# Steps of a fused long-convolution block: order of four engines where the pipeline has no FFN, on one core

## The reference

```python
def _L0_attn_ref(u, ...):                    # u: 2 x 4096 x 256, already layer-normed
    z = rmsnorm(u, pre_norm_w) @ in_proj_w.T     # then a causal depthwise conv of 3 taps
    x2, x1, v = jnp.split(z_pre, 3, axis=1)
    xv = x1 * v                                  # a long convolution along the 4096 rows
    y = (yconv + xv * D_skip[None, :, None]) * x2
    y = y @ out_proj_w.T + u
    zm = rmsnorm(y, post_norm_w)
    mlp = jax.nn.gelu(zm @ l1_w.T) * (zm @ l2_w.T) @ l3_w.T     # 672 hidden
    return y + mlp
def _L0_ffn_ref(x, W1, b1, W2, b2, scale):
    # m1, m2: outer products of rows 1 to 16 of each batch, added to W1 and W2
    h = einsum(x, W1) + scale * einsum(x, m1) + b1              # 1024 hidden
    h = jax.nn.gelu(h, approximate=False)
    return einsum(h, W2) + scale * einsum(h, m2) + b2
x = x + _layernorm(_L0_attn_ref(_layernorm(x)))
x = x + _layernorm(_L0_ffn_ref(_layernorm(x)))
```

## Time and profile before

| | |
|---|---|
| median of 3 runs | 1122.17 us (1121.68 to 1126.74) |
| profiled execution | 1130.82 us, span 1129.1 us |
| mean granted TensorE clock in it | 0.974 |
| ACT table loads | 64 |

### The profile page before, as it was taken

The page is one execution under the profiler, slowest core; times in us unless marked ns, Lnnn a source line. Parts: engine busy times, 40 slices in busy tenths (PEclk is TensorE's granted clock), DMA queues, the critical chain, the costliest instruction groups (busy, mean ns, idle before and its releaser), DMA issues.

```text
span 1129.1 us, 25540 instructions
## 1 busy us (share of the span) xinstructions
PE 1058.1 (94%) x9280; PEld 1026.8 (91%) x9280; DVE 880.7 (78%) x2313; ACT 724.5 (64%) x1607; POOL 295.2 (26%) x560
## 2 busy tenths in 40 slices
PE   4999999798678999999999999988999999999996
PEld 4899998576568999999999999988999999999996
DVE  7998998654368788888778888788778888877774
ACT  6888887555455666666666666565666566666553
POOL 6677674630010112111112111111111211111121
PEclk9999999889688999999999999998999999999999
DMA  3333321997743233443333344452333333333000
GB/s 123 114 122 118 108 75 39 273 252 196 136 78 66 38 57 48 51 56 66 57 57 48 49 53 65 90 123 38 59 55 57 49 49 52 56 62 57 26 14 29
DMA packets 108926, 89.23 MB, mean 79 GB/s; under 512 B 7121, under 2 KB 103537, under 8 KB 108545
## 3 DMA queue, kind: packets, MB, share of 16 engines
q1 hardware_dynamic: 107632, 85.16, 36.8%
q0 software_dynamic: 672, 2.39, 0.6%
q10 hardware_dynamic: 496, 0.05, 0.0%
HBM read 62.12 MB, written 17.07 MB: 70 GB/s over the span
## 4 chain that ended last, share of the span: by engine, by line
PE 66%; DVE 6%; DMA 4%; issue 3%; ACT 1%; POOL 1%; ACTq 0%; SPq 0%; DVEq 0%; POOLq 0%
PE ps_ring L1393 35%; PE ps_w L1393 14%; PE ps_m L1393 9%; PE ps_o L1393 3%; DMA toep<-taps_scratch 3%; PE ps_rt L1403 2%; PE ps_y L823 2%; PE ps_y L832 1%; DVE base L1249 1%; POOL sc L1017 1%; PE ps_m L1439 1%; DVE bn L1155 1%; PE ps_s L801 0%; DVE prod L1197 0%; DVE pt_l L1167 0%
## 5 line engine op out<-in xcount | busy, mean ns | idle before, releaser
L1017 POOL TENSOR_TENSOR sc<-sc,neg_half 128x2 f32<-128x2 f32 x128 | 95.5, 746 | 738.4 <-DVE sc L1348 449.7
L1077 ACT ACTIVATE gate<-ps_ring 128x256 f32<-128x256 f32 x192 | 73.2, 382 | 137.3 <-PE ps_ring L1393 136.2
L1393 PE MATMUL ps_ring<-mt_h,wl_h 128*128 128x256 f32 x640 | 130.6, 287 | 6.4 <-ACT mt_h L1144 6.4
L1393 PE MATMUL ps_ring<-mt_l,wl_h 128*128 128x256 f32 x640 | 130.3, 286 | 6.4 <-DVE mt_l L1167 6.4
L1098 ACT ACTIVATE hid<-ps_ring,b1s 128x256 f32<-128x256 f32 x256 | 114.0, 491 | 31.7 <-PE ps_w L1393 13.9
L1393 PE MATMUL ps_ring<-mt_h,wl_l 128*128 128x256 f32 x640 | 130.1, 286 | 0.0
L1167 DVE TENSOR_TENSOR ht_l<-hid,ht_h 128x256 fp32r<-128x256 f32 x256 | 103.2, 423 | 15.4 <-ACT ht_h L1102 9.5
L1393 PEld LDWEIGHTS ps_ring<-mt_h,wl_h 128*128 128x128 f32 x640 | 101.5, 196 | 7.7 <-ACT mt_h L1144 4.4
L1393 PEld LDWEIGHTS ps_ring<-mt_l,wl_h 128*128 128x128 f32 x640 | 101.3, 196 | 7.6 <-DVE mt_l L1167 7.6
L1393 PE MATMUL ps_ring<-xt_h,we_h 128*128 128x256 f32 x512 | 102.6, 282 | 2.3 <-DVE prod L1197 1.5
L1197 DVE TENSOR_TENSOR prod<-ps_ring,gate 128x256 f32<-128x256 f32 x192 | 80.9, 421 | 29.6 <-ACT gate L1077 25.7
(11 more groups left out here) (179 smaller groups left out, 2772.2 us busy)
## 6 DMA issues: line engine op xcount, KB each, us to landing
toep<-taps_scratch SPq DMA_DIRECT2D x30, 512.0 KB, 4.9
xa<-in_x SPq DMA_DIRECT2D x16, 512.0 KB, 4.5
x_scratch<-x2c SPq DMA_DIRECT2D x16, 512.0 KB, 3.5
x2s<-x_scratch SPq DMA_DIRECT2D x32, 256.0 KB, 6.9
xa_c<-in_x SPq DMA_DIRECT2D x32, 256.0 KB, 2.7
xb_c<-in_x SPq DMA_DIRECT2D x32, 256.0 KB, 2.7
out<-frow SPq DMA_DIRECT2D x32, 256.0 KB, 2.9
yin<-seq SPq DMA_DIRECT2D x124, 64.0 KB, 6.2
```

The source lines that it names most:

```text
L1017: nc.gpsimd.tensor_tensor(sc[:, to], sc[:, to], neg_half[:, 0, 0:CC], ALU.pow).then_inc(S[done], 1)
L1077: nc.scalar.activation(gate[rows_of, m % 2], ring[m % RING][rows_of, 0], ACT.Gelu_apprx_tanh).then_inc(S["gate_done"], 1)
L1393: mm = nc.tensor.matmul(out, lhs(a, kk), rhs(b, kk), start=(j == 0), stop=(closed and j == len(todo) - 1))
```

## The change

Three predicates name the steps: `bare` (0 and 1), `exposed` (0, 1, 2 and 18) and `second_sooner` (1). ScalarE: the exact gelu's table is loaded only in steps with a hidden part, the tanh gelu's not at all in bare steps, and behind the copy mt_h in steps -1, 2 and 18. VectorE: in bare steps yrow of the next unit is made ahead of the last block's low part; in exposed steps mt_l is made behind the add, ahead of its statistics. TensorE: in bare steps the turn of the scaled rows is done between the two chunks of the down projection. In step 1 the turn of the second norm's rows, its copy xt_h and its low part xt_l (with the two small instructions for odd) are moved between block 3 and block 4.

```diff
+        def bare(n):
+            return valid(n, UC) and not valid(n - FFN_AT, UC)
+        def exposed(n):
+            return bare(n) or (valid(n, UC) and late(n - FFN_AT))
+        def second_sooner(n):
+            return n == 1
...
@@ ScalarE
+                        if m == 3 and second_sooner(n):
+                            second_high(u)
-                    load_table(ACT.Gelu)
+                    if valid(h, UC):
+                        load_table(ACT.Gelu)
...
-                    load_table(ACT.Gelu_apprx_tanh)
+                    if valid(n, UC) and not exposed(n):
+                        load_table(ACT.Gelu_apprx_tanh)
                     act.wait_ge(S["zt_mm"], n + 2)
                     wait(act, S["ml_mm"], FB * (n + 1))
                     nc.scalar.activation(zt[0][:], ps_t[:], ACT.Copy).then_inc(S["zh_done"], 1)
+                    if not valid(n, UC) or (exposed(n) and not bare(n)):
+                        load_table(ACT.Gelu_apprx_tanh)
@@ VectorE
+                if second_sooner(n):
+                    second_low(u)
                 if valid(n, UC):
                     mlp_product(n, 4)
                     mlp_product(n, 5)
+                    if bare(n):
+                        with_rows(n + 1)
+                    product_low(n, FB - 1)
...
                     nc.vector.tensor_tensor(acc, ps_m[:], acc, ALU.add).then_inc(S["a_done"], 1)
+                    if exposed(n):
+                        turned_low(n + 1)
                     dve.wait_ge(S["a_done"], n + 1)
                     measure(acc, 0, "a_stat")
...
-                if valid(n + 1, UC):
-                    dve.wait_ge(S["zh_done"], n + 2)
-                    split_low(zt[1][:], ps_t[:], zt[0][:], "zl_done")
+                if valid(n + 1, UC) and not exposed(n):
+                    turned_low(n + 1)
@@ TensorE
                         mlp_block(n, m)
+                        if m == 3 and second_sooner(n):
+                            turn_second(u)
...
                 if valid(n, UC):
-                    mlp_down(n)
+                    mlp_down(n, 0)
+                    if bare(n):
+                        turn_scaled(n + 1)
+                    mlp_down(n, 1)
                 if valid(h, UC) and not late(h):
                     ffn_down(h, 0)
-                if valid(n + 1, UC):
+                if valid(n + 1, UC) and not bare(n):
                     turn_scaled(n + 1)
```

More of the change, by code:

```diff
@@ L1102, in hidden, with second_high @@
                         nc.scalar.activation(ht[0][:, 0], hid[:, 0], ACT.Copy).then_inc(S["hh_even"], 1)
+            def second_high(u):
+                act.wait_ge(S["xt_mm"], u + 1)
+                wait(act, S["h_mm"], HB * u)
+                nc.scalar.activation(xt[0][:], ps_t[:], ACT.Copy).then_inc(S["xh_done"], 1)
             for n in steps():
@@ L1123, in _ @@
                         last_norm(w, c)
[L1124 to L1127, removed]
+                if valid(u, UC) and not second_sooner(n):
+                    second_high(u)
                 if valid(n + 1, UC):
@@ L1200, in mlp_product @@
                     product_low(n, m - 1)
-                if m == FB - 1:
-                    product_low(n, m)
             def product_low(n, m):
@@ L1290, in output, with with_rows, turned_low, second_low @@
                                         ).then_inc(S["out_done"], 1)
+            def with_rows(n):
+                dve.wait_ge(S["xhat_done"], CC * (n + 1))
+                dve.wait_ge(S["o_mm"], n + 1)
+                nc.vector.tensor_tensor(yrow[:, n % 2], ps_o[:], xa[:], ALU.add).then_inc(S["yrow_done"], 1)
+            def turned_low(n):
+                dve.wait_ge(S["zh_done"], n + 1)
+                split_low(zt[1][:], ps_t[:], zt[0][:], "zl_done")
+            def second_low(u):
+                dve.wait_ge(S["xh_done"], u + 1)
+                split_low(xt[1][:], ps_t[:], xt[0][:], "xl_done")
+                if u % UCB == 0:
+                    scaled_odd(u // UCB)
             for n in steps():
@@ L1335, in _ @@
                     output(w)
[L1336 to L1340, removed]
+                if valid(u, UC) and not second_sooner(n):
+                    second_low(u)
                 if valid(n + 1, UC):
[L1342 to L1345, removed]
+                    if not bare(n):
+                        with_rows(n + 1)
                     dve.wait_ge(S["squared"], CC * (n + 2))
@@ L1430, in out_projection, with mlp_down @@
                 mm.then_inc(S["o_mm"], 1)
[L1432 to L1441, removed]
+            def mlp_down(n, c):
+                if c == 0:
+                    pe.wait_ge(S["pl_done"], FB * (n + 1))
+                    pe.wait_ge(S["stacked"], n + 1)
+                    wait(pe, S["a_done"], n)
+                product(ps_m[:, c], lambda a, m: pt[a][:, m, chunk(c)], lambda b, m: wl3[b][:, m], FULL, closed=False)
+                mm = nc.tensor.matmul(ps_m[:, c], pstack[:, chunk(c)], wstack[:], start=False, stop=True)
+                if c == CC - 1:
+                    mm.then_inc(S["m_mm"], 1)
             def ffn_up(h, n, first):
@@ L1492, in _ @@
                     ffn_up(h, n, first)
-                if valid(u, UC):
+                if valid(u, UC) and not second_sooner(n):
                     turn_second(u)
```

## The result

The changed kernel takes 1130.75 us (median of 20 runs, 1126.83 to 1136.82), the kernel before in the same measurement 1127.84 (median of 20, 1121.68 to 1131.56): ratio 1.0035, 95% interval 1.0022 to 1.0048. It is slower by 0.35%, inside the half per cent that I called no change. Of the three runs of before that were shown, two (1121.68 and their median, 1122.17) are the lowest of the 20.

A forecast was written before the change was run, and what follows sets the result against it. VectorE's chain was taken to bound the head, through step 3's fifth block on TensorE. +1.2 us after the first batch and +0.4 at step 18 made +1.6 on 1122.17: 1123.8 us, range 1119.3 to 1128.2.

The forecast's parts named there:

- the base: Whole kernel: 1122.17 us, the median time before the change, to which the summed effect of +1.6 us was added.
- An earlier restart did count only up to VectorE's first product: Head of the last stage: TensorE restarting sooner gains only until VectorE's first product; step 3's fifth block sets the gain.
- The rival of full gain: Whole head and step 18: TensorE's early restarts count in full, -11 us, 1111 us; chance 0.07.
- I take one short stretch: Step 1, behind a 3.1 us gap: one 3.4 us stretch at half clock, costing 1.5 us; add at 335.1.
- another short stretch: Step 3's fifth block, behind a 3.9 us gap: half clock costs +1.5 us, net +1.2 after the first batch.
- the slower rival: Steps 1, 3 and 18: each gap brings 6.8 us of half clock, costing 3.0 us; 1128.5 to 1130; chance 0.12.
- step 18: Where the second batch's weights are made: fifth block 0.6 us sooner, likely half clock +1.0, net +0.4 us.
- H: Experiments' theory, steps 1, 3 and 19: half clock behind TensorE's longer gaps costs the time; filler gains 4 to 6 us.
- V: Experiments' theory, steps 0 and 1: VectorE's own order costs the time; those edits alone give ratio 1.002 to 1.004.
- the rival in which it holds: Steps 1, 3 and 18: the clock doesn't fall behind the gaps, -2.4 us, 1119.8 us; chance 0.2.
- C: Experiments' theory, steady part: matmuls take 24.47 or 24.78 us a step by chance, making the 3.81 us and much spread.

The follow-up runs named there:

- e6: The changed kernel with 24 filler matmuls ahead of step 1's down projection alone; 1131.32 us.
- e4: The changed kernel with 24, 30 and 20 filler matmuls before step 1's down projection and the fifth blocks of steps 3 and 19; 1130.46 us, ratio 0.9988.
- e8: The kernel of e3 with 18, 14, 10 and 10 filler matmuls in the first block of steps 1, 2, 3 and 19; 1127.55 us, ratio 0.9976.
- e12: The kernel of e8 again, unedited, for a second profile; 1126.34 us (one run).
- e5: The changed kernel again, with no edit, on one chip with e6, e7 and e8; 1132.31 us, ratio 1.002.
- e3: The kernel before without the table loads of steps 0 and 1, and step -1's behind its copy; 1127.84 us, ratio 0.997.
- e2: The kernel before with only the change's edits of steps -1, 0 and 1; 1132.31 us, ratio 1.001.
- e11: The changed kernel a third time, with no edit, for another profile; 1135.64 us (one run).
- e7: The changed kernel with filler matmuls ahead of the fifth blocks of steps 3 and 19 alone; 1130.14 us.

## Why the prediction was right, and where it was wrong

The measured 1130.75 us lies above the range, 1119.3 to 1128.2. Two terms put it there: the base to which the sum was added, 5.7 us too low, and the length of the half-clock stretches in steps 1 and 3, taken as short.

**Right: the direction, no change within half a per cent, and what moved.** With 2.71 added, forecast and measured: step 0's down projection 309.74, 309.03; its add 314.07, 313.50; TensorE's restart 315.4, 314.84; step 1's first product 319.4, 318.83; its down projection 329.26, 328.66, behind a gap of 3.1, in fact 2.92; the gap in step 3 3.9, in fact 3.62. All are 0.3 us or less off once the 0.6 us by which step 0 was put too late is taken off. That 0.6 is in part luck of the two profiles: over three of each, the change has add 0 1.1 us later behind the stage's start than before (23.62 for 22.55 us), and the forecast had 0.8; the profile of before that was shown has the longest of its three. ScalarE's 60 loads, no half clock behind step 1's restart and the turn that waits for nothing are there too. An earlier restart did count only up to VectorE's first product. The first product of step 1 is 0.4 us ahead of its old place, where 0.3 was allowed. The rival of full gain falls: this product stands at 318.83, not before 318.5.

**Wrong: "I take one short stretch", and "another short stretch" in step 3.** These are the terms that were mis-sized. Both stretches lasted 6.8 us in all three profiles of the change. Step 1: from the down projection to the add 7.24 us (325.95 to 333.19) against 4.64 at full clock (e6, 325.60 to 330.24), so 2.6 for the 1.5 forecast; the 4.33 that the prediction had for full clock was 0.3 too low besides. The add stands at 335.90, forecast 335.1. Step 3: add 2 to add 3 is 2.5 us above what it is with the clock held (1.5 forecast). This is the mechanism of the slower rival for steps 1 and 3, to which I gave 0.12. Its own condition, the clock still at 0.50 when step 2's add comes, wasn't met: the stretch ended at 331.97, ahead even of step 1's add at 333.19, and step 2 itself paid nothing (26.10 us from add to add, 26.54 before). The price for a short stretch was right (1.4 and 1.3 measured, forecast 1.5); its length was the choice that failed. The earlier trace rows had two long stretches in three, and the one of step 19 in the same trace is long too.

Up to add 3 the forecast was +1.2 and the shown profiles give +3.37: step 1 +1.4 and step 3 +1.0 too little (half clock but for 0.3 of it), step 0 0.6 too much, the rest small terms. At step 19 (the place that the prediction calls step 18) the forecast was +0.4 and the two profiles give +0.48; but the three of the change have 85.79, 88.05 and 85.99 and the three of before 85.31, 84.11 and 85.28, a mean of +1.7.

**Wrong: the base.** I carried the difference over to 1122.17, the median of three runs. The median of 20 is 1127.84, 5.67 us higher, and 6.95 us are missing between 1123.8 and 1130.75: 5.67 of them are the base, 1.3 the change. The range was built on the bounds of the change alone, and took in nothing for what three runs leave open. That the profiled execution took 1130.82 should have warned me: I subtracted 8.65 us as if it were a property of the profile, when two of the 20 runs took as long, and 34 of 70 in the two later measurements of the kernel before. With the base of 20 runs the same sum gives 1129.4.

**Theories.** H holds in the profiles: three profiles of the change agree within 0.05 us from add 0 to add 3, filler at a place takes the half clock and its cost away there, and VectorE's order is untouched by it. In the timed runs it isn't shown step by step. V falls as the cause of the 81.0 us, with e4, e6 and step 1's earlier first product, but not altogether. With no half clock from add 0 to add 1, the change's order takes 19.81 us (e4, e6) and the old order without the loads 19.14 (e8, e12); up to add 3 it is 76.61, with one short stretch, for 75.12 and 74.69. So the new order gains nothing on the old one even where the clock is held, and the 2.4 us of the rival in which it holds don't come: from the yrow of step -1 to add 3 e4 takes 100.73 us, the kernel before 101.12, 99.02 and 100.12. C holds as to the steady part: e4 has the change's order and 318.07 us. The 3.81 us between the two profiles shown are thus no fixed cost of the change; whether the change shifts the odds of a cadence three profiles don't tell. That the cadence makes much of the spread between timed runs isn't shown.

**Open.** The three profiles of the change put it 1.1 us (to add 0), 3.5 us (add 0 to 3) and 1.7 us (16 to 19) above those of before, 6.3 us together, and the timed ratios say 3.9 and 2.3 us. An unprofiled run has no timeline, and short stretches in some of them would close this, but that isn't shown. Its mean granted clock says only that the change has no more half clock in all: 0.978 for it and for the kernel before beside e5. What differs is where the half clock falls. What sets the length of a stretch and what picks the cadence stay open as well. So does e3's 0.3%.

## What to carry to other kernels

Moving one engine's restart ahead of the work that bounds it didn't remove its wait, it gathered short waits into one long one: 1.86 and 0.96 us in step 1 became 2.92 in one piece, the 1.80 of step 3 became 3.62, and the half clock behind them fell on work that the end waits for. Price such a gap for both lengths of stretch that the trace shows, on the work that stands behind it, and try a little filler in it, in the old order as well as in the new one, before judging the change. Take the base from as many runs as the effect needs: three runs of a kernel that spreads over 10 us say nothing about 3.

## What the runs showed of the hardware that was not expected

With TensorE busy throughout at a granted clock of 1.00, a step takes 24.47 us in one execution and 24.55 and 25.01 us by turns in another of the same program. It stays so over most of a batch of weights: add 3 to add 16 was 318.07 us in three profiles of fourteen and 321.7 to 322.0 in ten, with one between (320.57). Add 19 to add 31 was 293.0 and 293.4 us in e6 and e2, and 295.4 to 296.3 in the other twelve. That is 3.8 us in 13 steps, as much as the change costs, and no row that I read separates the two: the granted clock is the same and the DMA share 0.36 against 0.35.

The other is that the clock's fall isn't told by the length of one gap. 3.60 us ahead of the same block brought a short stretch in e6 and a long one in e11, and 2.95 us ahead of step 1's down projection a short one in e7 and a long one in e5. The gap of 1.9 to 2.0 us ahead of step 0's down projection, in the seven profiles with the change's order there, brought a short stretch in two (e2, e7: 24.62 and 25.02 us to add 0) and none in five (23.45 to 24.12). The Trainium skill ("TensorE: Matmul & The Clock Gate", Part 1) says that the point of change is not tied to the kernel's start; the runs agree in that stretches which follow the same gap began 0.8 us ahead of the restart (the change, 369.52 for 370.27) or 1.2 us behind it (e6, 369.33 for 368.11).
